# State part turned by one more round: one batch's front beside another's attention chunks, half-head stages over one ring of six banks

## Time and profile before

| | us |
|---|---|
| median of 3 runs | 2973.41 |
| lowest, highest run | 2957.47, 2981.82 |
| profiled execution's own time | 2973.68 |
| its span | 2971.8 |
| PE busy | 2349.7 (79%) |
| DVE busy | 1966.0 (66%) |
| ACT busy | 1203.3 (40%) |
| POOL busy | 1201.9 (40%) |

### The profile page before, as it was taken

One profiled execution on the slowest core, in us unless ns is written; L12 is line 12 of the kernel. 1 busy time (PEld: TensorE's weight loads), 2 busy tenths in 40 slices (PEclk: granted clock), 3 DMA queues, 4 the chain that ended last, 5 costly groups with the idle time before them and its releaser, 6 DMA issues. The chain is left out here.

```text
span 2971.8 us, 51261 instructions
## 1 busy us (share of the span) xinstructions
PE 2349.7 (79%) x16440; PEld 1687.9 (57%) x16441; DVE 1966.0 (66%) x3521; ACT 1203.3 (40%) x2138; POOL 1201.9 (40%) x1332
## 2 busy tenths in 40 slices
PE   3488787878787878887888787878788884999990
PEld 1255555545554646464646464546464663999990
DVE  3685858485848585858585858485858543777777
ACT  2253434353535353535353535353535341333333
POOL 0233535353535353535353535353435343333336
PEclk8699898989998999899989998989998997999995
DMA  2000000000000000000000000000000003222116
GB/s 87 4 1 5 12 4 11 4 11 4 11 4 11 4 11 4 11 4 11 4 11 4 11 4 11 4 11 4 11 4 11 0 12 115 61 57 59 55 53 173
DMA packets 84508, 66.04 MB, mean 22 GB/s; under 512 B 10728, under 2 KB 78448, under 8 KB 84032
## 3 DMA queue, kind: packets, MB, share of 16 engines
q1 hardware_dynamic: 75984, 47.41, 5.6%
q0 software_dynamic: 8448, 17.58, 1.8%
HBM read 39.00 MB, written 27.03 MB: 22 GB/s over the span
## 5 line engine op out<-in xcount | busy, mean ns | idle before, releaser
L1307 DVE TENSOR_TENSOR_SCAN hs<-decay,push 128x512 f32<-128x512 f32 x256 | 369.6, 1465 | 5.6
L1062 ACT ACTIVATE sq<-banks 128x512 f32<-128x512 f32 x128 | 76.5, 598 | 633.6 <-PE banks L756 633.6
L1697 POOL TENSOR_TENSOR y<-y,ch 128x1024 f32<-128x1024 f32 x96 | 228.3, 2378 | 246.0 <-DVE ch L1314 245.3
L751 PE MATMUL banks<-qd,state 128*128 128x128 f32 x768 | 145.0, 348 | 191.2 <-DVE S L1401 111.2
L906 PE MATMUL banks<-rowsT,w_here 128*128 128x128 f32 x2176 | 269.9, 278 | 5.2 <-DVE w_here L1612 5.2
L1298 DVE TENSOR_TENSOR push<-du,banks 128x1024 f32<-128x1024 f32 x128 | 155.5, 1215 | 165.0 <-PE banks L669 164.8
L906 PEld LDWEIGHTS banks<-rowsT,w_here 128*128 128x128 f32 x2176 | 256.5, 194 | 8.5 <-issue 8.3
L751 PEld LDWEIGHTS banks<-qd,state 128*128 128x128 f32 x768 | 124.8, 247 | 198.5 <-DVE S L1401 115.8
L1845 POOL DMA_INDIRECT results_scratch<-rows_out,result_to x136 | 131.8, 969 | 239.0 <-ACT rows_out L1170 235.9
L1401 DVE TENSOR_TENSOR S<-banks,E 128x512 f32<-128x512 f32 x256 | 163.9, 681 | 82.7 <-PE banks L734 82.7
L1706 POOL TENSOR_TENSOR rstd<-var,minus_half 128x4 f32<-128x4 f32 x48 | 48.8, 1017 | 408.3 <-DVE var L1272 408.3
(11 more groups left out here) (232 smaller groups left out, 5625.8 us busy)
## 6 DMA issues: line engine op xcount, KB each, us to landing
rows_in<-rows_scratch SPq DMA_DIRECT2D x136, 66.0 KB, 1.8
both<-results_scratch SPq DMA_DIRECT2D x32, 256.0 KB, 3.4
w<-w_dram SPq DMA_DIRECT2D x3, 2048.0 KB, 8.0
x_tok<-x_dram SPq DMA_DIRECT2D x16, 256.0 KB, 2.8
x_scratch<-x SPq DMA_DIRECT2D x16, 256.0 KB, 2.3
tokens<-x_scratch SPq DMA_DIRECT2D x16, 256.0 KB, 2.8
out_dram<-final SPq DMA_DIRECT2D x16, 256.0 KB, 2.4
results_scratch<-rows_out,result_to POOLq DMA_INDIRECT x136, 2.3
```

Source lines behind the costliest of these rows:

```text
L751: pe.matmul(o_banks[:, f, h * P:(h + 1) * P], state[:, c % 2, 4 * f + h, :], qd[:, 4 * f + h, :], start=(h == 0), stop=False)
L1307: nc.vector.tensor_tensor_scan(hs[:, h, :], decay[:, n % 2, h, :], push[:, h, :], 0.0, ALU.mult, ALU.add).then_inc(s_scan, 1)
L1697: nc.gpsimd.tensor_tensor(y[:], y[:], ch[:, n % 2, :, :], ALU.add).then_inc(s_ysum, 1)
```

## The change

The round is turned by one more batch. `body(i, j, n)` now has attention of batch `j`, the states of batch `i = j + 1`, and the front of the state part (transposes, convolution, B/C/dt rows, gate, step sizes) of batch `n = j + 2`; there are 18 bodies instead of 17. The front stands beside the chunks, in the stages that `FRONT` names; in the first part of a round states 0 to 3 run, and states 4 to 7 in stages 0 to 3.

- **Stages.** The half chunks become eight stages `h`, the chunk `c = h // 2` and its half `f = h % 2`. In stage `h` PE does the update of half `h`, then `front(h + 1)` (falls `e`, `v`, output gates `og`, turned keys, masks, scores) for the next half, then steps of the other batches, `project_out` of the chunk before, and last `outputs(h)`. `S` has four slots and ACT's exp writes the mask into it, so `E` is gone.
- **One ring.** The two rings of three banks become one ring of six, in the one order that `ring_uses` lists.
- **B and C.** The 16 rows of a batch are stored to DRAM, and SP loads each spread over 128 partitions (16 loads of 256 KB a batch) into two slots of `b_all` and of `c_all`; `push` and `ch` read them there. The matmuls, the bfloat16 parts and their DVE operations go. dt is read in float32 from the same tile `xd`.
- **y.** DVE starts `y` with `xc * D + ch` of state 0 (`start_sum`, two operations). States 1 to 6 are added by DMAs that accumulate in SBUF, issued by GpSimd, each behind the one before; state 7 by DVE in `gate_state`.
- **Squares.** GpSimd no longer sums them; PE runs eight matmuls against ones per chunk instead of one.
- **Moved between engines.** The state's decay goes from GpSimd to ACT (16 copies of 128x128 a round, with a scale per partition), the copy `take` from DVE to ACT, all of q is drained by ACT (two of eight were DVE's), `chunk_fall` is an exp on ACT. GpSimd decays queries by half (six a round of 128x512 instead of three of 128x1024).
- **Logarithms.** The Ln of the state part's step sizes is now apart from that of attention's decay.

```diff
+    for h in range(2 * TILES):
+        c, f = divmod(h, 2)
+        uses += [("attention", f"U{f}_{c}")] if c < TILES - 1 else []
+        uses += [("attention", use) for use in (front_uses(h + 1) if h + 1 < 2 * TILES else ())]
+        uses += [("state", use) for use, stage in STATE_OUT.items() if stage == h]
+        uses += [("front", use) for use, stage in FRONT.items() if stage == h]
+        uses += [("attention", f"wo_{c - 1}")] if c and f == 0 else []
     return uses
...
-L0_STEPS = [[3], [4], [], [2], [5], [], [6], [7], [8], [9], [10], [11], [12, 13], [14], [15], []]
...
-Q_BY_DVE = (2, 3)
...
+SCANS_IN_UNIT = {1: 1, 3: 2, 5: 3}
+PRODUCTS_IN_UNIT = {2: 1, 4: 2, 6: 3}
+STATE_IN_STAGE = {0: 4, 1: 5, 2: 6, 3: 7}
...
+SUMS = STATES - 2
+STATE_OUT = {"mix": 4, "x1T": 6, "ffn": 6}
+FRONT = {"xT": 0, "u0": 1, "u1": 2, "xdbl": 3, "z0": 5, "z1": 5, "dt0": 6, "dt1": 6}
+SIZES_STAGE, BC_STAGE, TAKE_STAGE, X3_AFTER = 7, 3, 2, 3
...
-            body(0, None)
-            body(1, 0)
-            with eng.Fori(2, B) as r:
-                body(r, r - 1)
-            body(None, B - 1)
+            body(None, None, 0)
+            body(0, None, 1)
+            body(1, 0, 2)
+            with eng.Fori(3, B) as r:
+                body(r - 1, r - 2, r)
+            body(B - 1, B - 2, None)
+            body(None, B - 1, None)
...
+                slot = n % BC_SLOTS
+                if n == 0:
+                    sp.wait_ge(s_bc_stored, at(i, 16, 16))
+                if n >= BC_SLOTS:
+                    sp.wait_ge(s_push, at(i, STATES, n - BC_SLOTS + 1))
+                sp.dma_start(b_all[:, slot, :], bc_dram[bass.ds(i, 1), n].broadcast_to([P, T])).then_inc(s_b[slot], 16)
...
-                    for c, row in (("B", n), ("C", STATES + n)):
-                        bank, full = fill(l0, f"{c}{n}", i)
-                        pe.matmul(bank, sel[:, row, :], parts[:], start=True, stop=True).then_inc(full, 1)
...
-                pe.wait_ge(s_ssum, at(j, 3 * TILES, 3 * c + 3))
-                pe.matmul(bank[:, P:P + 1], sq[:, 0, 0:P], ones[:, 0:1], start=True, stop=True).then_inc(full, 1)
+                for t in range(PAIRS):
+                    mm = pe.matmul(bank[:, P:P + 1], sq[:, t // 4, t % 4 * P:(t % 4 + 1) * P], ones[:, 0:1],
+                                   start=(t == 0), stop=(t == PAIRS - 1))
+                mm.then_inc(full, 1)
...
+            def stage(h, i, j, n):
+                c, f = divmod(h, 2)
+                if j is not None:
+                    if c < TILES - 1:
+                        update(h, j)
+                    if h + 1 < STAGES:
+                        front(h + 1, j)
+                if i is not None:
+                    if h == STATE_OUT["mix"]:
+                        state_out(i)
+                    if h == STATE_OUT["x1T"]:
+                        turn_mixed(i)
+                    if h == STATE_OUT["ffn"]:
+                        sign_ffn(i)
+                if n is not None:
+                    if h == FRONT["xT"]:
+                        turn_input(n)
+                    for half in range(HALVES):
+                        if h == FRONT[f"u{half}"]:
+                            convolve(half, n)
+                    if h == FRONT["xdbl"]:
+                        parameters(n)
+                    for half in range(HALVES):
+                        if h == FRONT[f"z{half}"]:
+                            gate_input(half, n)
+                    for half in range(HALVES):
+                        if h == FRONT[f"dt{half}"]:
+                            step_size(half, n)
+                if j is not None:
+                    if c and f == 0:
                         project_out(c - 1, j, j)
+                    outputs(h, j)
...
+            def start_sum(i):
+                if not first(i):
+                    dve.wait_ge(ring.full_sem("mix"), ring.full_at("mix", i - 1))
+                dve.wait_ge(s_ch, at(i, STATES, 1))
+                for h in range(HALVES):
+                    nc.vector.scalar_tensor_tensor(y[:, h, :], xc[:, h, :], d_skip[:, h:h + 1], ch[:, 0, h, :],
+                                                   ALU.mult, ALU.add).then_inc(s_ystart, 1)
...
+            def gate_state(i):
+                dve.wait_ge(s_ysum, at(i, 16 * SUMS, 16 * SUMS))
+                dve.wait_ge(s_ch, at(i, STATES, STATES))
+                for h in range(HALVES):
+                    nc.vector.tensor_tensor(y[:, h, :], y[:, h, :], ch[:, (STATES - 1) % 2, h, :], ALU.add
+                                            ).then_inc(s_ygate, 1)
...
+            def stage(h, i, j, n):
+                m = STATE_IN_STAGE.get(h) if i is not None else None
+                if j is not None:
+                    if h:
+                        gate_out(h - 1, j)
+                    add_update(h, j)
+                state_part(m, 1, i)
+                if j is not None and h + 1 < STAGES:
+                    decay_keys(h + 1, j)
+                state_part(m, 2, i)
+                if j is not None and h + 1 < STAGES:
+                    mask_scores(h + 1, j)
+                state_part(m, 3, i)
+                if m is not None and m + 1 < STATES:
+                    state_part(m + 1, 0, i)
+                if j is not None:
+                    if h == 0 and not first(j):
                         index_rows(j - 1)
+                    if h % 2 and h > 1:
+                        residual((h - 3) // 2, j)
+                if i is not None:
+                    if h == GATE_STAGE:
+                        gate_state(i)
+                    if h == MIX_STAGE:
+                        add_mixed(i)
+                    if h == NORM_STAGE:
+                        normalize(x1, s_rstd0, s_x1, i)
+                if n is not None:
+                    for half in range(HALVES):
+                        if h == FRONT[f"u{half}"]:
+                            convolved(half, n)
+                if i is not None:
+                    if h == FFN_STAGE:
+                        add_ffn(i)
+                    if h == NORM2_STAGE:
                         normalize(x2_new, s_rstd1, s_x2, i)
+                if n is not None:
+                    for half in range(HALVES):
+                        if h == FRONT[f"z{half}"]:
+                            gate_input(half, n)
+                    if h == SIZES_STAGE:
+                        step_sizes(n)
...
-                        nc.gpsimd.tensor_tensor(y[:], y[:], ch[:, n % 2, :, :], ALU.add).then_inc(s_ysum, 1)
...
+                pool.sem_inc(s_sum_begun, 1)
+                nc.gpsimd.dma_start(y[:], ch[:, n % 2], accum_op=ALU.add).then_inc(s_ysum, 16)
```

1071 lines of the change are left out of this document (528 added, 543 removed).

## The result

The changed kernel takes 2618.98 us (median of 4 runs, 2611.19 to 2623.08) where the kernel before took 2974.77 (4 runs): a ratio of 0.8808, 95% interval 0.8765 to 0.8852. The forecast was 2680 us in a range of 2525 to 2840. The profiled execution took 2623.08 us, its span is 2621.2.

A forecast was written before the change was run, and what follows sets the result against it. Before, hand-offs left 21 us of PE waits in the chunks' part; after, the larger of PE and DVE sets each stage. First opening 128, 15 rounds of 130, last round 112, experts 488, 1.9 around: 2680 us, range 2525 to 2840.

The forecast's parts named there:

- Stages 0 to 6: Chunks' part of a round: the larger of PE's and DVE's time in each stage, the shorter engine hidden.
- first part of a round: Projections after an opening: 42 us, 3 us over the longer of PE's 38.7 and DVE's 37.5.
- The clock: Chunks' part: of 8 us for pieces that ran at half clock, 4 us a round left in, with fewer waits.
- The seam: Round's end: 3 us added, as x2's squares on ACT stand behind step sizes with two table loads.
- One accumulating DMA: Sum of a state into y, 512 KB: 5.0 us and 1 for its issue, bounds 3.5 to 18.
- Scans were to fall to 1.2 us: DVE's state scans: 1.2 us each, from a mean of 1465 ns, as GpSimd's sums are gone.
- the margin of 3 us over the longer engine: First part of a round: 42 us taken against 38.7 of PE, where it was 5.5 over before.
- (a): Stages: hand-offs don't overlap, 1 to 2 us more wait a stage, round likely 142, 2860 us; chance 0.17.
- (b): GpSimd and DVE meet more, push and ch beside half qd: 8 us, round 138, 2800 us; chance 0.06.
- (d): Faster: squares at their lower end, no seam, clock held; round about 118, 2500 us; chance 0.08.
- (c): Slower: chain of y sums bounds the round, deciding from 11.5 us a sum; 3265 us at 18; chance 0.08.
- The cover of the last sum: Last sum into y lands 58 us behind the opening, gate_state wants it at 84: hidden by 26 us.

The follow-up runs named there:

- squares_bf16: The changed kernel with squares written as bfloat16 and summed by the same eight matmuls against bfloat16 ones: 2528.57 us, ratio 0.8496.
- front_late: The changed kernel with front(h + 1) moved behind outputs(h), next to its use, nothing added or left out: 2809.72 us, ratio 0.9413.
- hint: The changed kernel with a prefetch hint for the branch that closes the loop over rounds, on each engine: 2579.86 us, ratio 0.8653.
- bf16_hint: The changed kernel with both bfloat16 squares and the prefetch hint at the loop's end: 2518.79 us, ratio 0.8426.
- fall_dve: The changed kernel with attention's two decay subtractions done by DVE instead of GpSimd: 2594.34 us, ratio 0.8688.
- squares_gpsimd: The changed kernel with a chunk's squares summed by GpSimd again and one ones-matmul on PE instead of eight: 2633.62 us, ratio 0.8843.
- sum_halves: The changed kernel with each accumulating DMA of 512 KB issued as two of 256 KB, one behind the other: 2827.59 us, ratio 0.9474.
- y_gpsimd: The changed kernel with states 1 to 6 added into y by GpSimd instead of accumulating DMAs: 2725.17 us, ratio 0.9157.
- sum_twice: The changed kernel with every accumulating DMA issued twice, the second behind the first (output not the reference's): 2957.62 us, ratio 0.9947.

## Why the prediction was right

**The bound and the step that decides it.** The forecast rested on PE setting the stages once each front stands a stage ahead. Stages 0 to 6 were to take 76.5 us (the larger of PE and DVE) and took 76.60. PE's pieces alone were forecast at 77.8 - 2.0 = 75.8 us for them, and PE was busy 75.76. squares_bf16 shows the bound from the other side, where PE's saving arrives nearly whole, and front_late shows the condition: with the front next to its use half the gain is gone. The close agreement of the sum is in part luck. Stage 0, where DVE's 8.5 us were to decide, took 7.75, PE's time (DVE's rest ran over into stage 1, where PE waited 0.16 us for it), and stage 6 took 13.67 and not 12.6, of which 0.68 is PE's wait for x1's turned copy (L753 for ACT).

**The terms of the sum.**

| | forecast | measured |
|---|---|---|
| first opening | 128 | 127.3 |
| first part of a round | 42 (PE 38.7, DVE 37.5) | 43.4 (PE 36.0, DVE 37.4) |
| stages 0 to 6 | 76.5 | 76.6 |
| stage 7 and seam | 4.7 + 3 | 4.9 |
| lower clock | 4 | none in stages 0 to 6; in the first part it is inside the 43.4 |
| other rounds against that one | | 1.1 longer in the mean |
| a round | 130 | 126.0 |
| last round | 112 | 115 |
| mixture of experts | 488 | 489 |

Two terms were mis-sized, the clock and the seam. They make 2.9 and 2.8 us of the round too much; the first part, 1.4 too little, gives some of it back, and 4 us a round are left by which the forecast was high.

*The clock, 4 us.* I carried half of the old loss over. In stages 0 to 6, where PE's waits are 0.8 us in all, the granted clock is 1.00. What is left stands behind the opening (clock 0.96 in the first part, 0.50 from 1263.30 to 1265.00), and in a few rounds (129.2 and 131.2 us between 1511.9 and 1772.4, at a clock of 0.95 and 0.92, where the one before them has 0.97).

*The seam, 3 us and DVE's stage 7.* I let x2 be late by ACT's chain and let DVE set stage 7. PE's last outputs ended at 1383.2, the last norm at 1383.8, and PE began at 1385.89: x2 had been ready for 2.1 of the 2.7 us of idle time, and these are the loop's turn, which hint takes away (0.67 us of wait for x_new stay). Stage 7 took 2.2 us, PE's time and not DVE's 4.7. The 3 us of the seam were near by luck, as the cause was another; the chain that I named appears only when PE is shorter (bf16_hint).

**Where it was right for the numbers given.** Squares: 1.5 us a chunk more; eight take 1.71 where one took 0.14. Four table loads a round, as counted. B/C loads land in 5.3 us and not 2.8, and are hidden as said, since `push` idles 0.1 us in all. One accumulating DMA: 5 + 1 us taken, 5.1 to 7.4 measured.

**Where a reason failed inside a right number.** Scans were to fall to 1.2 us because GpSimd's sums go. They fell to 1406 ns: in the first part two pairs meet attention's decay on GpSimd and take 3.71 and 3.78 us (fall_dve). That is 2.8 us more DVE work than forecast, and still DVE is busy 37.4 us there for the 37.5 forecast: other work of it came out as much shorter, and this agreement is luck. The part came out 1.4 us longer than forecast, while PE is busy 36.0 us in it and not 38.7; the margin of 3 us over the longer engine had to be 6.

**The rivals.** (a) no: hand-offs in the stages cost 0.8 us in all. (b) in its kind, neither in its place nor in its size: it put the contention at push and ch beside qd, which never meet, and it is in the scans of the first part, 2.8 us a round and not 8. (d) no, though the clock held in the stages, as it had it. (c) did not come true, and its price was worked out from the wrong mechanism. I named the work that GpSimd's queue holds, but priced only a chain of sums that decides from 11.5 us for one; what decides first is that GpSimd stands in a wait with other engines' work behind it, and that comes sooner: splitting each DMA in two, with the same bytes, costs 12.5 us a round while `gate_state` has nothing to wait for. The cover of the last sum was wrong too. It was to land 58 us behind the opening, 26 us ahead of the gate. It was issued at 1333.15, 72.1 us behind the opening, since a sum also waits for its `ch` and for the scatters ahead of it in GpSimd's queue; at the 7.4 us of the first of them it lands at 79.5 us, and the gate's add starts at 83.4. That is an estimate of some 4 us of cover, from these rows.

**What stays open.** How much of the gain is the turned round itself, a batch's front beside another's chunks, was not taken apart: no kernel was run that has the new stages without the turn. Nor was B/C by DMA undone by itself. Known is what it costs to take the order out of the finished kernel (0.061), what y by DMA is worth (0.035 in it, 0.013 in the kernel before), and that in stages 0 to 6 PE's busy time is nearly all of the time. These shares need not add up, as the two worths of y by DMA show.

## What to carry to other kernels

Price a new order stage by stage from the pieces of the trace: here five of seven stages came out within 0.3 us, the two others 0.8 under and 1.1 over. Here it held while what one engine makes for another stood a full stage ahead; to undo that alone cost half of this gain (0.061 of 0.119). Once an engine is full, try first to make its cheapest work cheaper in place: for the squares that was worth 93 us (squares_bf16), while moving them to GpSimd put them behind its scatters, where PE waited 49.0 us for them and nothing was gained (squares_gpsimd). And look twice at a wait for a transfer in a queue that also holds work for others, however idle that queue's engine looks: GpSimd was busy 32% of the span in sum_halves, and a round was 12.5 us longer.

## What the runs showed of the hardware

- Eight ones-matmuls of one column took 1.71 us in float32, which are sixteen passes of 0.11 us, and 0.21 us in bfloat16, eight of 0.026 us (squares_bf16).
- At the turn of the loop over rounds (some 860 matmuls a round) PE was idle 2.8 us in the mean of 12, and projections behind it ran at half clock (L772 1.91 and 1.80 us, later 1.02); with `hint_back_edge=True` on the loop that idle time is gone and a round is 3.4 us shorter (hint).
- A pair of 128x512 scans took 2.34 us alone and 3.71 beside one GpSimd subtraction of 112x512 that itself lasts 1.48 (changed kernel). A GpSimd add of 128x1024 took 2.36 us alone and 3.16 beside a VectorE product with both inputs in SBUF that keeps its 1.22 (y_gpsimd).
- An accumulating DMA within SBUF took 3.8 to 6.0 us for 256 KB and 5.1 to 7.4 for 512 KB, with its issue (sum_halves, sum_twice): half the bytes saved a fifth to a quarter of the time.
